# Order of the value products and number of probability tiles in a fused attention kernel

## The reference

```python
# first attention: 16 heads of 16, linear bias by distance, causal
scores = einsum('bhqd,bhkd->bhqk', Q, K) / sqrt(hd) + alibi
attn = softmax(where(causal, scores, -inf), axis=-1)
out = einsum('bhqk,bhkd->bqhd', attn, V)
# second attention: rotary, 16 query heads on 4 key/value heads, causal
scores = einsum('bhqd,bhkd->bhqk', q, k) * scale
probs = softmax(where(causal, scores, min), axis=-1)
attn = einsum('bhqk,bhkd->bqhd', probs, v)
```

## Time and profile before

| what | us |
|---|---|
| median of 3 runs | 2557.66 (2552.64 to 2558.59) |
| profiled execution | 2548.83 |
| its span, first to last instruction | 2547.0 |
| attention, first product of step 0 to the end of step 15 | 369.0 to 1961.5 |
| a steady step (1 to 14) | 96.9 to 97.2 |
| PE, DVE, ACT busy over the span | 91%, 76%, 60% |

### The profile page before, as it was taken

One profiled execution on the slowest core, in us unless ns is written; L12 is line 12 of the kernel. 1 busy time (PEld: TensorE's weight loads), 2 busy tenths in 40 slices (PEclk: granted clock), 3 DMA queues, 4 the chain that ended last, 5 costly groups with the idle time before them and its releaser, 6 DMA issues. The chain is left out here.

```text
span 2547.0 us, 50665 instructions
## 1 busy us (share of the span) xinstructions
PE 2317.4 (91%) x16370; PEld 1233.6 (48%) x16371; DVE 1924.3 (76%) x5054; ACT 1518.9 (60%) x3292; POOL 583.0 (23%) x845
## 2 busy tenths in 40 slices
PE   3599988999999999999999999999999874999997
PEld 2355553344444444444444444444443652788886
DVE  7777759999999999999999999999992663333332
ACT  2133314677778778777787787787787551222221
POOL 6412102121111111111111111111000356332223
PEclk8799998999999999999999999999999996999999
DMA  4167775454343443322322322322122884334433
GB/s 156 70 194 218 210 187 91 78 109 80 68 84 75 72 79 71 64 53 56 58 56 52 65 56 46 71 56 46 33 77 66 291 288 156 69 76 76 77 74 70
DMA packets 168155, 246.60 MB, mean 97 GB/s; under 512 B 52120, under 2 KB 124968, under 8 KB 162100
## 3 DMA queue, kind: packets, MB, share of 16 engines
q0 software_dynamic: 38304, 112.51, 23.5%
q1 hardware_dynamic: 124596, 121.03, 16.1%
q10 hardware_dynamic: 5044, 10.32, 1.4%
HBM read 120.38 MB, written 122.36 MB: 95 GB/s over the span
## 5 line engine op out<-in xcount | busy, mean ns | idle before, releaser
L1405 ACT ACTIVATE a_p<-banks 128x512 f32<-128x512 f32 (+3 forms) x2560 | 1176.5, 541 | 320.3 <-PE banks L1287 188.7
L1456 DVE TENSOR_REDUCE a_mx<-banks 128x1 f32<-128x512 f32 x1536 | 966.3, 683 | 64.3 <-PE banks L1275 52.1
L1368 PE MATMUL banks<-a_p,a_v 128*32 128x512 f32 (+3 forms) x5120 | 598.4, 542 | 1.0 <-ACT a_p L1405 0.5
L1453 DVE CUSTOM_DVE_ANT_0 a_masked<-banks,a_later 128x128 bf16<-128x128 f32 (+3 forms) x1024 | 452.9, 485 | 45.6 <-PE banks L1275 33.0
L1275 PE MATMUL banks<-a_k,a_q 48*128 48x512 f32 (+7 forms) x1600 | 336.2, 427 | 15.6 <-ACT a_p L1405 3.9
L1287 PE MATMUL banks<-a_q,a_k 50*128 50x512 f32 (+7 forms) x1600 | 330.1, 422 | 16.2 <-ACT a_p L1405 5.0
L1275 PEld LDWEIGHTS banks<-a_k,a_q 52*128 52x128 f32 (+1 forms) x1600 | 153.3, 184 | 224.7 <-DVE a_mx L1456 118.1
L1287 PEld LDWEIGHTS banks<-a_q,a_k 54*128 54x128 f32 (+1 forms) x1600 | 151.6, 184 | 218.6 <-DVE a_mx L1456 130.5
L2148 ACT ACTIVATE e_hT<-banks 128x256 fp32r<-128x256 f32 x72 | 27.6, 383 | 310.9 <-PE banks L2074 280.1
L1275 PE MATMUL banks<-a_k,q 48*128 48x512 f32 (+7 forms) x896 | 189.3, 431 | 9.4 <-DVE a_mx L1453 1.3
L2087 PE MATMUL banks<-w,e_hT 128*128 x576 | 185.2, 424 | 12.2 <-DVE e_hT L2188 12.2
(11 more groups left out here) (267 smaller groups left out, 2573.2 us busy)
## 6 DMA issues: line engine op xcount, KB each, us to landing
expert_rows<-a_zeros POOLq DMA_DIRECT2D x132, 258.0 KB, 5.3
a_k<-ka_parts POOLq DMA_DIRECT2D x42, 256.0 KB, 6.3
e_x<-expert_rows SPq DMA_DIRECT2D x72, 129.0 KB, 2.8
expert_rows<-e_y SPq DMA_DIRECT2D x72, 128.0 KB, 2.0
qa_parts<-m_part SPq DMA_DIRECT2D x16, 512.0 KB
ka_parts<-m_part SPq DMA_DIRECT2D x16, 512.0 KB, 4.9
va_tiles<-m_va SPq DMA_DIRECT2D x8, 1024.0 KB, 4.7
qb_parts<-m_part SPq DMA_DIRECT2D x16, 512.0 KB, 4.7
```

Source lines behind the costliest of these rows:

```text
L1368: ins = pe.matmul(ps_o[VW * h:VW * h + VW, c0:QB], v_op[o][:, kt, hk * VW:hk * VW + VW], prob[:, (n * GH + h) % NPB, c0:QB], start=(kt == ...
L1405: nc.scalar.activation(prob[:, (2 * n + j) % NPB, c0:QB], ps[(slot + j) % RING][:, c0:QB], ACT.Exp, scale=SCALE).then_inc(s_ex, 1)
L1453: ins = v.tensor_tensor_reduce(masked[:, turn + j, 0:w], ps[banks[j]][:, 0:w], later[:, WIDE - w:WIDE], 1.0, MASKED, ALU.add, ALU.max, top)
L1456: ins = v.tensor_reduce(top, ps[banks[j]][:, 0:w], AX.X, ALU.max)
```

## The change

`prob` gets 20 tiles instead of 16, and of each two value products (0 and 1, 2 and 3, ...) the first moves later in the order, to directly ahead of the second, which stays where it was. So all 40 of a step stand in runs of two: 20 runs instead of 39 in `ORDER`, and 20 instead of 37 in `FIRST_ORDER`. All other letters keep their order: with the v taken out, the old and the new strings are the same. The tile index gets the step's share (`t * NSC`, a multiple of 160, so of 16 and of 20).

```diff
-NPB = 16
+NPB = 20
...
 ORDER = (
-    "smvsmsssmvmsmsvmsmvmsmvsmsmsmvmsmvssmsmvsmsvsmsmsvmsmvsmmvmssvmsmvssmvmsmsvsmsmvmsmmsmvs"
-    "mmrtsmsvsmmvsmsvmmsvssmsmsmvsmmrvtsmsvmmsmvsmssmvmsmsvsmmsmsmvmsstrmsmvsmsvmsmvsmvmssvms"
-    "ssmvmsmsmvmsmvmssvmssmsmsvvmssrt"
+    "smsmsssmvvmsmsmsmvvmsmsmsmsmvvmsmssmsmvvsmssmsmsvvmsmsmmvvmssmsmvvssmmsmsvvsmsmmsmmsmvvs"
+    "mmrtsmssmmvvsmsmmsvvssmsmsmsmmrvvtsmsmmsmvvsmssmmsmsvvsmmsmsmmsstrmsmvvsmsmsmvvsmmssvvms"
+    "ssmmsmsmvvmsmmssvvmssmsmsvvmssrt"
 )
...
 FIRST_ORDER = (
-    "mmmmmmmmrmmmmmmmmmsmmsmmsmsmmsvmmmmrvmmsmmmsmsmmsmvvsmmmvsmsmsmmvsmsmmmsvsmsmsvmsmrtsmms"
-    "vmmvsmmsvvmsmsmmsvsmsmmvsmsmvsmmsmsmvsmsmmsmvsmsmmssvmmsvmmsmsmmrmsmmvsmsvmmmsvmmvssmmvs"
-    "msvmmsmmvsmrmsmsvssmmvmsmmsvmsmsmvsmsmsmrvsmsmvsmsvmsmsvstsmsvmsmsmvsmsmvsssmmvsmsvvmsst"
+    "mmmmmmmmrmmmmmmmmmsmmsmmsmsmmsmmmmrvvmmsmmmsmsmmsmvvsmmmsmsmsmmvvsmsmmmssmsmsvvmsmrtsmms"
+    "mmvvsmmsvvmsmsmmssmsmmvvsmsmsmmsmsmvvsmsmmsmsmsmmssvvmmsmmsmsmmrmsmmvvsmsmmmsvvmmssmmvvs"
+    "msmmsmmvvsmrmsmsssmmvvmsmmsmsmsmvvsmsmsmrsmsmvvsmsmsmsvvstsmsmsmsmvvsmsmsssmmvvsmsvvmsst"
     "tr"
 )
...
                             ins = pe.matmul(ps_o[VW * h:VW * h + VW, c0:QB], v_op[o][:, kt, hk * VW:hk * VW + VW],
-                                            prob[:, (n * GH + h) % NPB, c0:QB], start=(kt == 0),
+                                            prob[:, (t * NSC + n * GH + h) % NPB, c0:QB], start=(kt == 0),
...
-                    nc.scalar.activation(prob[:, (2 * n + j) % NPB, c0:QB], ps[(slot + j) % RING][:, c0:QB],
+                    nc.scalar.activation(prob[:, (t * NSC + 2 * n + j) % NPB, c0:QB], ps[(slot + j) % RING][:, c0:QB],
```

## The result

The changed kernel takes **2870.29 us** (median of 4 runs, 2855.01 to 2873.49), the kernel before 2557.84 beside it: ratio **1.1213** (1.1193 to 1.1234), 312 us more. The direction was right, the size was not: the forecast was 2670, with a range up to 2725. The profiled execution is 2867.38, 318.5 above that of before.

The account below looks back on a forecast made before the run. DVE, busy 89.8 of a 97 us step, was taken as the floor, coupled to PE and ACT by the ring. Fourteen steps +112, step 0 +4.4, last step 0: +116, giving 2670 us, range 2615 to 2725.

Parts of the forecast that it names:

- What bounds the kernel: Steady step of 97 us: DVE busy 89.8, a floor; the ring of seven banks couples PE, DVE and ACT, none free.
- PE's saving: Each run of products that disappears saves PE about 0.32 us, at most 6.1 a steady step; counts only where DVE waits.
- PE bounds, the drains go: Rival: PE's 6.1 us a step come off in full, 2453 to 2462 us; chance 0.04 together with a half-size form.
- I take 105.1 for the step: Steady step: DVE's 89.8 plus 14.1 us forced idleness, plus up to 2.8 elsewhere; 8.0 us more, +112 over fourteen steps.
- the count: Sum of idle time an order forces on DVE behind product runs: 14.1 us a steady step new, 4.6 old.
- DVE and ACT run dry in turn: Rival: behind runs both start empty and PE waits for either's banks; 109 us a step, 2725 to 2735; chance 0.13.
- The clock stays at 1.00 in the attention: Expected profile sign: PE's granted clock remains at its full level in the attention; no time was added for it.
- Step 0 and the last step: Step 0: forced idleness 3.4 to 7.8 us, +4.4; last step: 0, between -2 and +3.
- Twenty tiles: Five groups instead of four may be open; no wait in either order, 0 us.
- The profile's marks: Signs expected: step near 105, DVE busy 89.8, ACT 77.3, full run about 1.9, idle stretches 0.3 to 1.3 us.

Follow-up runs that it names:

- short_second_old_order: Kernel before with twenty tiles, old orders, the second of each two products cut to 64 query columns except a block's last: 2709.97 us, one execution.
- short_second: Changed kernel with the second product of each two cut to its last 64 query columns, except a query block's last: 2717.62 us, one execution.
- tiles_only: Kernel before with twenty tiles and the new index, both orders as before: 2549.41 us against 2548.20, ratio 1.0006.
- experiment 15: Kernel before with twenty tiles, second products cut to 64 columns, first matmul of each maximum pair done twice: 2748.38 us, one execution.

## Why the prediction was right and wrong

**What bounds the kernel: right.** DVE's busy time per step is nearly the same in every kernel (89.3 to 91.7), and every loss is its idleness. PE's saving was real and worth nothing: a full run takes 1.85 us as forecast, yet PE stands without a matmul for 11.1 us of step 2 in place of 3.0, and 8 us less of PE's work in short_second_old_order left the step at full clock at 97.2. The rival *PE bounds, the drains go* is dead. The Trainium skill's sentence on PSUM (TensorEngine Tiling (Array Packing), PSUM Bottleneck) was a better guide than what it says of drains (Key Properties on the same page).

**The term "I take 105.1 for the step": mechanism right, size off.** short_second shows the mechanism (109.4 to 98.7 with the runs cut short). At full clock it is between 106.5 (97.1 + 9.4) and 109.4, so +9.4 to +12.3 in place of +8.0. Behind the runs, at the 19 of 20 places that are seen at full clock, DVE idles for 15.7 us where the count says 12.9; with the clock's part its idle time is 27.2 in all. The prediction had noted that its formula errs low at the one place of the old order that it worked through (0.24 for 0.58), and added nothing for it. Its working there also took 0.88 for a lone product, which is the price of one followed by another; with 1.00 it gives 0.36. The likely reason for the rest is that the count assumes a full ring at each run's start: the excess is 0.25 us a place where runs stand close, and 0.03 elsewhere. The rival *DVE and ACT run dry in turn* put the full-clock step at 109; its 0.13 was too little, though even its 2735 was 135 below the result. Whether the two engines ran dry in turn, or each by itself, was not separated.

**The sentence "The clock stays at 1.00 in the attention": wrong, and the costliest.** It stood among the marks and in no term of the sum. With 22.4 us a step at half clock it cost 7.5 to 10.4 us a step, 105 to 145 over fourteen; step 0 (0.89 to 0.75) became 26.8 longer, not 4.4, and the last step 10.1, not 0, at 0.94. The sentence had no reason beside it. The profile of before gave a hint: step 0 was at 0.89 there, so PE in this kernel is not beyond the reach of the lower clock, and the change lets it work less and wait more.

**Step 0 and the last step** were mis-sized with it: 37 us in place of 4.4. An estimate with the slope of 0.34: step 0 has 2 x 0.25 x 181.3 - 2 x 0.11 x 154.5 = 57 us more at half clock, 19 of its 26.8, and the last step 2 x 0.06 x 89.2 = 11, 4 of its 10.1. That leaves about 7 for the order in step 0, where 4.4 was forecast, and 6 in the last step, where nothing was. No run separates them.

**Twenty tiles: right**, 0 us (tiles_only). **The profile's marks:** DVE busy for 89.8, ACT for 77.3, the idle stretches released by L1275, all seen; the run near 1.9 and idle stretches of up to 1.3 us, seen at full clock only, and with some up to 1.55 (3.57 and 2.51 at the lower clock); waits of 13 and 23 us or more for DVE and ACT: seen (14.5 and 23.1 for the largest line of each in step 2).

So the 318.5 us are about 130 to 170 of starvation in the fourteen steps, 105 to 145 of the clock in them, 37 in the first and last step from both, and 3.8 behind the attention.

**Open.** What activity of PE keeps the clock at 2.4 GHz was not found. A filler that raises it for nothing was not found either, so the clock's share rests on slopes within profiles, on the two steps of experiment 15 and on equal runs met at either level, and not on a run that changes the clock alone. Why the second attention's steady steps of the changed kernel have more half-clock time than the first's (27.8 us in the mean against 17.1) was not tested; before, neither has any.

## What to carry to other kernels

Where one engine feeds two others through a ring of banks, its work for neither of them belongs where their backlog is full, in pieces that are smaller than that backlog, and with enough pairs in between to fill it again; here two pieces with one pair between cost as much as two that touch. A count of forced idleness from a static order ranks places, and in sum it was too low here. Before PE's work is cut or bunched in a kernel where PE waits for others, read the granted clock by stretch: the saved work can come back as a lower clock and cost more than it saved.

## What the runs showed of the hardware

- With about 8 us less work a step on PE and the order as before (short_second_old_order), the granted clock fell from 1.00 to a mean of 0.83 in the steady steps (35.4 of 107.1 us at half), and the kernel went from 2549 to 2710 us.
- The clock falls without any long gap in PE's work: in the few microseconds ahead of the 60 falls in the steady steps of the changed kernel a matmul was in flight for 0.81 to 0.87 of the time, by how many are taken, against 0.91 in its mean, and the largest gap between matmuls there is 0.49 us. The kernel before has gaps of up to 0.68 us in its steady steps, with a matmul in flight for 0.97 of them, and no fall.
- The falls keep to places: in the changed kernel nine of the twenty runs of a step met full clock in all fourteen steady steps, and the run of products 26 and 27 met it in none.
- A microsecond at 1.2 GHz cost these kernels 0.28 to 0.47 us, not half or more. DVE and ACT take nearly as long for their work: 90.3 and 78.4 us in the step of short_second_old_order at 0.73, 89.8 and 77.3 in the old kernel's at 1.00. A run of two full products takes 1.85 us at one level and 3.57 at the other (changed kernel), a lone one 1.00 and 1.86 (short_second_old_order).
